# A product of the state-space loop moves from VectorE to GpSimd, and another one moves one unit later

## The reference, cut to what matters

```python
def fp_step(y_prev):
    x_tilde = (x - y_prev) @ W_mix.T + y_prev          # called u in the kernel
    bc = _shift1(y_prev) @ W_bc.T
    Bt = bc_normalize(B0 + bc[..., :D_STATE])
    Ct = bc_normalize(C0 + bc[..., D_STATE:])
    y = _selective_scan(x_tilde, delta, A, Bt, Ct, D)  # h = exp(dt*A)*h + (dt*u)*B; y = h.C + D*u
    return layer_norm(y)
y_star = fori_loop(0, 8, lambda i, y: y + STEP * (fp_step(y) - y), y0)
```

## Time and profile before

| | us |
|---|---|
| median of 3 runs | 10106.7 |
| lowest and highest | 10106.22, 10123.09 |
| the profiled execution | 10121.23 |
| its span | 10119.3 |

### The profile page before, as it was taken

The page is one execution under the profiler, slowest core; times in us unless marked ns, Lnnn a source line. Parts: engine busy times, 40 slices in busy tenths (PEclk is TensorE's granted clock), DMA queues, the critical chain, the costliest instruction groups (busy, mean ns, idle before and its releaser), DMA issues.

```text
span 10119.3 us, 254917 instructions
## 1 busy us (share of the span) xinstructions
PE 9191.3 (91%) x86530; PEld 6259.2 (62%) x86530; DVE 8675.3 (86%) x16668; ACT 7116.7 (70%) x14939; POOL 6113.9 (60%) x4900
## 2 busy tenths in 40 slices
PE   7999899998999989999899999999989999999998
PEld 4656656566565665656656566565665656656566
DVE  6988979789797897978979799797997979979798
ACT  5867768677686776857768577685776858668586
POOL 1946829368293772937729377292773927739286
PEclk9999999999999999999999999999999999999999
DMA  1000000100001000010000000000000000000000
GB/s 40 1 21 1 2 20 0 21 1 5 17 0 21 1 5 17 0 21 1 5 17 0 21 1 7 15 0 21 1 9 13 0 21 1 15 7 0 21 1 3
DMA packets 690788, 95.10 MB, mean 9 GB/s; under 512 B 633594, under 2 KB 684989, under 8 KB 685245
## 3 DMA queue, kind: packets, MB, share of 16 engines
q1 hardware_dynamic: 690237, 88.00, 6.7%
HBM read 60.26 MB, written 25.22 MB: 8 GB/s over the span
## 4 chain that ended last, share of the span: by engine, by line
PE 33%; DVE 28%; issue 15%; ACT 10%; POOL 10%; DVEq 2%; DMA 1%; POOLq 0%; SPq 0%; ACTq 0%
DVE work L1667 10%; POOL work L1786 10%; DVE work L1657 8%; ACT scan_in L1174 5%; PE ps L684 5%; PE ps L674 4%; PE ps L669 4%; PE ps L897 3%; PE ps L593 3%; PE ps L887 3%; PE ps L570 3%; PE ps L605 2%; DMA hend<-work 1%; ACT yscT L1207 1%; DVE du L1622 1%
## 5 line engine op out<-in xcount | busy, mean ns | idle before, releaser
L1786 POOL TENSOR_TENSOR work<-work,crep 128x512 f32<-128x512 f32 x4608 | 5762.2, 1276 | 3936.6 <-DVE work L1606 3445.6
L1174 ACT ACTIVATE scan_in<-du,bcn 128x256 f32<-128x256 f32 x8832 | 3691.7, 499 | 33.0 <-DVE bcn L1588 3.0
L1667 DVE TENSOR_TENSOR_SCAN work<-da,hend,ps 128x256 f32<-128x256 f32 x4608 | 3026.1, 725 | 32.3 <-PE ps L897 23.4
L897 PE MATMUL ps<-w_ident,scan_in 128*128 128x128 f32 x18432 | 2483.0, 278 | 383.4 <-ACT scan_in L1174 244.8
L897 PEld LDWEIGHTS ps<-w_ident,scan_in 128*128 128x128 f32 x18432 | 2012.4, 142 | 1009.8 <-issue 387.2
L1657 DVE TENSOR_TENSOR_SCAN work<-da,ps 128x512 f32<-128x512 f32 x2048 | 2354.1, 1202 | 53.6 <-issue 24.7
L887 PE MATMUL ps<-work,w_sel 128*32 128x256 f32 x17792 | 1382.9, 392 | 164.6 <-POOL work L1786 164.1
L1095 ACT ACTIVATE work<-ps,w_gate_b 128x512 f32<-128x512 f32 x512 | 351.5, 687 | 814.5 <-PE ps L669 760.2
L887 PEld LDWEIGHTS ps<-work,w_sel 128*32 128x32 f32 x17792 | 356.2, 108 | 646.9 <-POOL work L1786 388.0
L1407 DVE TENSOR_REDUCE smax<-ps 128x1 f32<-128x512 f32 x1024 | 642.1, 684 | 99.0 <-PE ps L570 98.8
L1061 ACT ACTIVATE da<-ps 128x512 f32<-128x512 f32 x1024 | 585.4, 598 | 185.3 <-PE ps L593 169.3
(11 more groups left out here) (201 smaller groups left out, 11655.2 us busy)
## 6 DMA issues: line engine op xcount, KB each, us to landing
da<-parts_d SPq DMA_DIRECT2D x192, 192.0 KB
hend<-work SPq DMA_DIRECT2D x2304, 1.0 KB, 1.8
parts_d<-scan_in SPq DMA_DIRECT2D x80, 256.0 KB, 2.2
da<-pad_d SPq DMA_DIRECT2D x32, 208.0 KB
da<-pad_d SPq DMA_DIRECT2D x32, 192.0 KB
x_in<-in_x SPq DMA_DIRECT2D x17, 256.0 KB, 2.8
out<-work SPq DMA_DIRECT2D x16, 256.0 KB
gate_w<-in_gate_w SPq DMA_DIRECT2D x1, 1024.0 KB, 4.9
```

The source lines that it names most:

```text
L897: mm = eng.transpose(ps[:, bank, c:c + P], scan_in[:, m, tb, 2 * j + s].rearrange("p k c -> p (k c)"), ident[:])
L1174: ins = eng.activation(scan_in[:, m, tb, :, k, :], du[:, hf, tb, :].rearrange("p (e c) -> p e c", c=GC), ACT.Copy, scale=bcn[:, hf, tb, 0, ...
L1667: ins = eng.tensor_tensor_scan(hst[:, p % NHID, half], da[:, 1, 2 * p + s, :], ps[:, RING[p % 4], half], hend[:, 2 * p + s:2 * p + s + 1], ...
L1786: eng.tensor_tensor(prod[:, to, :].rearrange("p (s t) -> p s t", s=2), hst[:, p % NHID, :].rearrange("p (s t) -> p s t", s=2), crep[:, hf, ...
```

## The change

In the half-1 unit POOL makes `du` of half 0 from `u_sb`, behind its product of p = 9; DVE no longer makes it there, and does its `front_norm` behind p = 10 instead of 11. ACT's copy of u to `u_sb` then waits for `u_done` instead of `du_done`, and (in both units) for the last reader of `u_sb` on POOL, `skip_done`. POOL's `skip` of half 0 moves from behind p = 11 of the half-1 unit to behind p = 5 of the half-0 unit. The half-0 unit's own `du` (of half 1) stays on DVE and its `skip` behind p = 11.

```diff
-POOL_SKIP = 11
+POOL_DU, POOL_SKIP, POOL_LATE, DVE_BCN_1 = 9, 11, 5, 10
...
             def front_keep(at, hf, kf):
-                eng.wait_ge(du_done.sem, du_done.count(at, kf + 1))
+                if hf == 1:
+                    eng.wait_ge(du_done.sem, du_done.count(at, kf + 1))
+                else:
+                    eng.wait_ge(u_done.sem, u_done.count(at, kf + 1))
+                eng.wait_ge(skip_done.sem, skip_done.count(at, kf))
                 eng.activation(u_sb[:], half6, ACT.Copy).then_inc(u_copied.sem, u_copied.up(at))
...
-                        if p == DVE_DU:
+                        if p == DVE_DU and hf == 0:
                             front_du(at, other, kf)
-                        if p == DVE_BCN:
+                        if p == (DVE_BCN_1 if hf else DVE_BCN):
                             front_norm(at, other, kf)
...
         @block.gpsimd
         def _(eng):
+            def front_du(at, hf, kf):
+
+                eng.wait_ge(u_copied.sem, u_copied.count(at, kf + 1))
+                eng.tensor_tensor(du[:, hf], u_sb[:], delta[:, hf * HB:(hf + 1) * HB, :],
+                                  ALU.mult).then_inc(du_done.sem, du_done.up(at))
+
...
-                    if p == POOL_SKIP and kf is not None:
-                        skip(at, 1 - hf, kf)
+                    if p == POOL_DU and hf == 1 and kf is not None:
+                        front_du(at, 0, kf)
+                    if p == POOL_LATE and hf == 0:
+                        skip(at, 0, 0)
+                    if p == POOL_SKIP and hf == 0:
+                        skip(at, 1, kf)
```

## The result

The changed kernel takes 10162.12 us (median of 5 runs, 10161.42 to 10162.22); the kernel before, run beside it, 10107.39. The ratio is 1.005, with a 95% interval of 1.0039 to 1.0061: 55 us or 0.54% slower. The forecast was 10192 us, slower by 85, in a range of 10110 to 10225. The direction and the place are right; the forecast size is half as large again as the measured one, and 10162 is nearer to rival B's 10145 than to the forecast.

The account below looks back on a forecast made before the run. POOL's chain through PE and ACT to y, not DVE alone, was taken to bound the turn. Late skip +0.80, du kept -0.13, wait +0.03 gave +0.70 us per turn, 85 us in all: 10192 us, range 10110 to 10225.

Parts of the forecast that it names:

- rival B: Half-1 unit: POOL's products 4 to 11 run at 1.24 us, not 1.32; at most +0.3 us per turn, 10145; chance 0.08.
- The late skip: POOL's half-0 unit: skip behind product 5 adds 1.29 us, 0.49 idle absorbs part; product 15 and y 0.80 us later.
- What is kept of DVE's du: DVE, half-1 unit: removing du saves 0.58 us per turn, of which only 0.13 to 0.14 is kept.
- the slack at the statistics: Half-0 unit's statistics on DVE: they could start 0.14 us earlier before waiting for POOL's product 15 chain.
- Where DVE waits: DVE idles about 0.5 us ahead of half-1 statistics and of y, 0.3 to 0.5 ahead of half-0 statistics.
- front_norm ahead of scan 11: DVE, half-1 unit: doing front_norm one step earlier costs nothing.
- The fill: ACT's fill of the half-0 unit's first steps comes a microsecond earlier, worth nothing as the statistics wait for POOL.
- The sum: One turn: +0.80 - 0.13 + 0.03 = +0.70 us; 85 us in all.
- The wait for u: POOL's du, half-1 unit: waiting for ACT's copy of u loses 0.03 us, bounds 0 and 0.3.
- rival C: POOL idles for u or du takes 1.5 us: +0.9 to +1.2 us per turn, 10222 to 10260; chance 0.08.

Follow-up runs that it names:

- the two kernels without `du`: Kernel before, neither engine making du of half 0 in the loop: 1.0047 with front_norm behind scan 10, 0.9946 with it behind scan 11.
- `skip` 1 in the next unit: Changed kernel with D u of half 1 made behind product 6 of the next half-1 unit, not product 11 of the half-0 unit: 0.9979, 10090.51 us.
- the kernels with 4922 and 4976 us outside their turns: Changed kernel without the late skip (4922): 10059.72 us; changed kernel with D u of half 1 made in the next half-1 unit (4976): 10090.51 us.

## Why the prediction was right or wrong

**What bounds.** The unbroken chain from POOL's product 7 in the half-0 unit through PE and ACT to y was read rightly: the last piece of the turn is 10.93 us before, 10.92 after and 10.93 with the late skip alone, whatever product 15's lateness. That DVE's 45 of 46 busy us don't set the turn alone is shown by the two kernels without `du`: 0.58 us less on DVE gave 0.23 us, or a loss. But in the half-1 unit, from product 7 to 15, I read POOL's row as one without a gap and so as POOL's own chain, and that was wrong: there DVE's scans hold product 15, with POOL close behind.

**The late skip, forecast +0.80.** Right, a little large: +0.70 in its piece, 0.63 in the turn between the kernels with and without it. A `skip` takes 1.25 us on POOL's timeline from start to next start, not 1.29, as neighbours overlap.

**What is kept of DVE's du, forecast 0.13.** This is the step that was mis-sized. The changed kernel has 0.21 + 0.11 = 0.32 us. The 0.11 was forecast as 0.14, the slack at the statistics. There the slack was larger: they start 2.70 us behind the end of product 15 where they started 2.98, but the scan behind them then waits 0.24 us for PE's transposes, and 0.11 reach product 4. The 0.21 was not in the sum: I set POOL's chain in the half-1 unit as fixed, "the same count of work as before", and took its 1.32 us products for POOL's own speed. They are paced by DVE's scan steps, 1.28 us from start to start (3034.36 to 3039.49, four steps). Rows of the kernel before, of scan 10, product 10, scans 12 to 15, scan 14, and products 13, 14 and 15, each looked up alone:

```profile
3031.24 0.72 DVE L1667 TENSOR_TENSOR_SCAN work<-da,hend,ps 128x256 f32<-128x256 f32 x1
3032.16 1.27 POOL L1786 TENSOR_TENSOR work<-work,crep 128x512 f32<-128x512 f32 x1
3034.36 5.21 DVE L1667 TENSOR_TENSOR_SCAN work<-da,hend,ps 128x256 f32<-128x256 f32 x8
3036.93 1.36 DVE L1667 TENSOR_TENSOR_SCAN work<-da,hend,ps 128x256 f32<-128x256 f32 x2
3037.16 1.27 POOL L1786 TENSOR_TENSOR work<-work,crep 128x512 f32<-128x512 f32 x1
3038.49 1.28 POOL L1786 TENSOR_TENSOR work<-work,crep 128x512 f32<-128x512 f32 x1
3039.72 1.27 POOL L1786 TENSOR_TENSOR work<-work,crep 128x512 f32<-128x512 f32 x1
```

Product 10 starts 0.20 us behind the end of scan 10 (3031.96) and product 14 as much behind that of scan 14 (3038.29), though POOL had ended product 13 at 3038.43; product 15 follows at once and ends at 3040.99. Merged into one row, these short waits can't be seen. Work put behind product 9 instead of 11 makes POOL late two products sooner, and products then run at 1.24 us: two of them 0.08 us quicker are 0.16 of the 0.21 us. Rival B had seen the 0.08 us, took it for five products and gave no cause; it expected 0.40 to 0.54 us kept. The run with `du` behind product 10 fits (12.73 us, between 12.86 and 12.65).

**Where DVE waits, forecast 0.5 us ahead of the statistics and 0.5 ahead of y.** It is 0.30 and 0.23. y's wait didn't grow, because DVE had lost 0.37 us to shorter waits on the way from the statistics to y. The 0.3 to 0.5 us forecast ahead of the half-0 unit's statistics did not come; DVE waits 0.24 us for PE behind them.

**front_norm ahead of scan 11, forecast nothing.** Right here, but by a cover that I didn't name. It holds scan 11 back 0.6 us, and is free only because POOL is behind by then; without `du` on POOL it cost 0.53 us a turn (46.41 against 45.88).

**The fill, forecast worth nothing.** Right at `POOL_DU` = 9. One product later it was 0.4 us a turn.

**The sum.** -0.21 - 0.11 + 0.70 - 0.01 for the rest is +0.37 us in place of +0.70, about 41 us over the 112 intervals, for 85. That the median grew by 55 and the profiled execution by 41 comes from the kernel before, whose executions differ by 17 us (10106.22 to 10123.09) where the changed one's differ by 1. Their time goes with the granted clock: in 28 executions of it on another chip, from 10124.5 us at 0.979 of full speed to 10106.7 at 0.983. The profiled one had 0.980. The clocks of the others beside the changed kernel aren't on record, so for these 14 us the clock is likely and not shown. The range held, but partly by luck: the error of 0.33 us a turn is nearly as large as the 0.37 measured.

**The wait for u.** Right: `du` starts 0.04 us behind product 9's end, for 0.03 us lost in the forecast, and ACT's copy stands 2.45 us nearer to product 7, for 2.4; rival C did not come.

## What to carry to other kernels

Busy shares don't say which engine sets a loop: cut the turn at fixed events, follow the chain through all engines, and ask of each piece what its neighbour's wait would be. A group of instructions that is a few per cent slower than its like may be paced by a producer, with waits too short to be listed; looking up single instructions shows them. Then work put in early is partly free, and work that holds the producer back is not. A third operation on an engine cost 0.63, 0.38 or 0 us by where it stood (behind product 5, behind product 3, and with the other `skip` moved into an idle stretch), so the place is to be chosen by the idle time behind it and not by the engine's share.

## What the runs showed of the hardware

The granted TensorE clock behind the loop differed from kernel to kernel, and with 18 transposes, 2.4 us of PE's work, put into the last unit of each sequence it was 1.00 there. They brought 17 us over 16 sequences in one kernel (10121.93 to 10105.04) and 37 to 50 in another. Two levels exist, 1.2 and 2.4 GHz; a mean of 0.78 over 15 us is some of each. How long PE stands doesn't tell the kernels apart: for the last two sums of the fifth sequence it stands 1.01 and 1.91 us in the kernel before, 1.01 and 1.90 in the changed one, 1.00 and 1.91 without the late skip, 0.95 and 1.94 with `skip` 1 in the next unit. In the same order, the two 15 us stretches there have a clock of 0.94 and 0.84, 0.99 and 0.90, 1.00 and 1.00, 0.88 and 0.78. What makes the difference is open. An experiment that moves the end of a stage can so gain some 30 us or lose some 20 far from its edit, as the kernels with 4922 and 4976 us outside their turns; comparing turns and whole times side by side brings that out.
